# Attention's first batch sent in halves of heads, stacks gathered by term, and a new order of its first stages

## The reference, cut to what matters

```python
qkv = hidden_states @ w_attn + b_attn
q, k, v = jnp.split(qkv, 3, axis=-1)
scores = jnp.einsum('bqhd,bkhd->bhqk', q, k) * SCALE
scores = jnp.where(causal[None, None], scores + bias[None], -jnp.inf)
attn = jax.nn.softmax(scores, axis=-1)
out = jnp.einsum('bhqk,bkhd->bqhd', attn, v).reshape(B, S, HIDDEN)
return out @ w_proj + b_proj
```

## Time and profile before

| what | value |
|---|---|
| median of three runs | 691.1 us (690.16 to 693.39) |
| the profiled execution's own time | 689.53 us |
| its span, first to last instruction | 687.8 us |
| PE busy | 647.3 us, 94% of the span |
| DVE, ACT, POOL busy | 482.1, 343.7, 86.5 us |
| mean granted TensorE clock | 0.995 of full speed |
| chain that ended last | PE 77%, DVE 15%, ACT 3%, DMA 1% |

### The profile page before, as it was taken

How to read it: one execution, slowest core, us unless ns; L and a number is a source line. 1 busy time by engine, 2 the same in 40 slices (tenths; PEclk the granted TensorE clock), 3 DMA queues, 4 the chain that set the end, 5 groups by cost and what they waited for, 6 DMA issues and landing times.

```text
span 687.8 us, 10297 instructions
## 1 busy us (share of the span) xinstructions
PE 647.3 (94%) x3848; PEld 490.8 (71%) x3848; DVE 482.1 (70%) x913; ACT 343.7 (50%) x539; POOL 86.5 (13%) x185
## 2 busy tenths in 40 slices
PE   4888999999998799999998999999999899999997
PEld 4866678678676577877787675766857565788876
DVE  6755685795689789886797556465374797787565
ACT  5213554614633764423479897476384904445221
POOL 4411002102100021101042010000100310000000
PEclk9999999999999999999999999999999999999999
DMA  8395513413644130000260000000003106000000
GB/s 278 109 262 169 155 32 96 131 54 94 224 146 169 66 140 26 0 1 1 92 225 13 1 0 1 0 1 0 1 0 117 67 1 229 2 31 16 15 31 32
DMA packets 31908, 52.15 MB, mean 76 GB/s; under 512 B 3449, under 2 KB 17148, under 8 KB 30303
## 3 DMA queue, kind: packets, MB, share of 16 engines
q1 hardware_dynamic: 31282, 49.84, 22.4%
q10 hardware_dynamic: 576, 1.64, 1.0%
HBM read 42.87 MB, written 8.40 MB: 75 GB/s over the span
## 4 chain that ended last, share of the span: by engine, by line
PE 77%; DVE 15%; ACT 3%; DMA 1%; issue 1%; ACTq 1%; POOL 1%; SPq 0%; DVEq 0%; POOLq 0%
PE ps L2021 15%; PE ps L1857 13%; PE ps L1890 12%; PE ps L2089 11%; PE ps L1720 5%; DVE nmax L1100 3%; PE ps L1798 2%; PE ps L1736 2%; PE ps L1866 2%; PE ps L1700 2%; DVE nmax L1097 2%; PE ps L1788 2%; DVE prodT L1623 2%; ACTq L508 1%; PE ps L1859 1%
## 5 line engine op out<-in xcount | busy, mean ns | idle before, releaser
L2089 PE MATMUL ps<-wdT,prodT 128*128 128x512 f32 (+1 forms) x176 | 77.7, 597 | 0.4
L2089 PEld LDWEIGHTS ps<-wdT,prodT 128*128 128x128 f32 (+1 forms) x176 | 32.8, 190 | 40.7 <-issue 38.3
L817 ACT ACTIVATE probsT<-ps 128x1536 f32<-128x1536 f32 x32 | 46.2, 1450 | 28.1 <-PE ps L1788 27.9
L859 ACT ACTIVATE funs<-ps 128x512 f32<-128x512 f32 x16 | 9.5, 596 | 92.0 <-PE ps L1859 80.6
L683 POOL TENSOR_SCALAR ln_spread<-ln_moments 128x1 f32<-128x1 f32 x24 | 7.5, 310 | 283.1 <-DVE ln_moments L1171 283.0
L1177 DVE SCALAR_TENSOR_TENSOR junk<-x_sb,gate_row 128x512 f32<-128x512 f32 x48 | 41.2, 858 | 1.0
L1623 DVE COPY prodT<-ps 128x512 f32<-128x512 f32 (+1 forms) x24 | 13.7, 599 | 37.0 <-PE ps L2076 36.7
L1440 DVE SCALAR_TENSOR_TENSOR x_sb<-b_row,coef,x_sb 128x512 f32<-128x512 f32 x48 | 38.0, 792 | 1.8
L1100 DVE TENSOR_REDUCE nmax<-ps 128x4 f32<-128x1024 f32 x32 | 38.9, 1214 | 0.0
L989 ACT ACTIVATE sign_junk<-mlp_size_next,minus_guess 128x1376 bf16<-128x1376 f32 x24 | 34.6, 1443 | 0.8
L989 ACT ACTIVATE sign_junk<-mlp_size_main,minus_guess 128x1376 bf16<-128x1376 f32 x24 | 34.6, 1442 | 0.7
(11 more groups left out here) (302 smaller groups left out, 1726.9 us busy)
## 6 DMA issues: line engine op xcount, KB each, us to landing
cuts<-parts SPq DMA_DIRECT2D x16, 384.0 KB, 2.8
qst<-cuts SPq DMA_DIRECT2D x48, 128.0 KB, 2.7
w_first_raw<-in_L_ffn_w SPq DMA_DIRECT2D x6, 1024.0 KB, 7.5
w_second_raw<-in_L_ffn_w SPq DMA_DIRECT2D x6, 1024.0 KB, 8.6
kst<-cuts SPq DMA_DIRECT2D x36, 128.0 KB, 2.6
wqkv_raw<-in_L_attn_a_w_attn SPq DMA_DIRECT2D x3, 1024.0 KB, 7.9
wdT<-in_L_attn_b_w_down SPq DMA_DIRECT2D x1, 2560.0 KB, 10.0
wg_raw<-in_L_attn_b_w_gate SPq DMA_DIRECT2D x1, 2048.0 KB, 8.4
```

Of the source, the lines that this page charges most:

```text
L817: nc.scalar.activation(probsT[:, g % 2, :].rearrange("p (k n) -> p k n", k=3), slot[g % 2], ACT.Exp).then_inc(exp_ok.sem, 1)
L2089: last = nc.tensor.matmul(ps[:, Y_BANK, :], prodT[0:m, c, :], wdT[0:m, c, :], start=(c == 0), stop=(c == IC - 1))
```

## The change

The first batch's steps go in the order f = 0, 1, 2, 3, so that both sides of the first half of the heads come first. SP writes and gathers that half while the second is still being cut; ACT issues no gathers any more. The columns of q and k are ordered so that a pair of heads lies side by side, and a row in DRAM has 1024 bytes where it had 512. The writes of q are three DMAs with a broadcast source, which put part 0 three times, part 1 twice and part 2 once (768 KB for a half); k is written once (384 KB). The gather of q is then one DMA to 96 partitions (768 KB), that of k three, to 48, 32 and 16 partitions (384, 256, 128 KB). So each half has four writes and four gathers, where it had two and twelve; this holds for all batches.

The transposed rows get two sets of buffers, by odd and even batch, so `turn_rows(1)` goes ahead of the values of batch 0 (into PSUM banks 0 and 1), and `turned_part(1, 1)` goes between the groups 1 and 2 of the first batch's scores. `residue(1, 0)` and `residue(1, 1)` go behind the maxima of groups 1 and 3. `cut_biases` and its DMAs go behind the values and the gathers of batch 0. Core of the diff:

```diff
+TERM_RUNS = [(0, 3, 0), (3, 2, 1), (5, 1, 2)]
...
-    turned = np.arange(D).reshape(2, H // 2, HD).transpose(0, 2, 1).reshape(D)
+    turned = np.arange(D).reshape(2, H // 4, 2, HD).transpose(0, 2, 3, 1).reshape(D)
...
-        cuts_out = [sig(f"cuts_out{half}", 16 * 2) for half in range(2)]
-        SCATTERS = 2 * len(TERMS)
+        WRITES = 1 + len(TERM_RUNS)
+        cuts_out = [sig(f"cuts_out{half}", 16 * WRITES) for half in range(2)]
+        SCATTERS = 1 + len(TERM_RUNS)
         scat = [sig(f"scat{half}", 16 * SCATTERS) for half in range(2)]
...
-        cuts = nc.dram_tensor("cuts", (2, 2, 3, D // 2, S), BF16, kind="Internal").ap()
+        q_cuts = nc.dram_tensor("q_cuts", (2, len(TERMS), P, 2 * S), BF16, kind="Internal").ap()
+        k_cuts = nc.dram_tensor("k_cuts", (2, 3, P, 2 * S), BF16, kind="Internal").ap()
...
+        def write_side(eng, b, half, side):
+            need(eng, part3, b, 2 * half + side + 1)
+            if side == 1:
+                eng.dma_start(k_cuts[half].rearrange("m p n -> p m n"),
+                              parts[:, 1, half].rearrange("p m g t -> p m (g t)")).then_inc(cuts_out[half].sem, 16)
+            else:
+                for t, n, part in TERM_RUNS:
+                    eng.dma_start(q_cuts[half, t:t + n].rearrange("m p n -> p m n"),
+                                  parts[:, 0, half, part].rearrange("p g t -> p (g t)").unsqueeze(1)
+                                  .broadcast_to([P, n, 2 * S])
+                                  ).then_inc(cuts_out[half].sem, 16)
+
         def send_rows(eng, b, half, side):
 
-            stack = (qst, kst)[side]
             hs = slice(half * H // 2, (half + 1) * H // 2)
-            for t, term in enumerate(TERMS):
-                eng.dma_start(stack[t:TROWS:len(TERMS), hs, :],
-                              cuts[side, half, term[side]].rearrange("(d h) t -> d h t", d=HD)
+            if side == 0:
+                eng.dma_start(qst[0:TROWS, hs, :].rearrange("r h t -> r (h t)"),
+                              q_cuts[half].rearrange("m (d h) n -> (m d) (h n)", d=HD)
                               ).then_inc(scat[half].sem, 16)
+            else:
+                for t, n, _ in TERM_RUNS:
+                    eng.dma_start(kst[t * HD:(t + n) * HD, hs, :].rearrange("r h t -> r (h t)"),
+                                  k_cuts[half, 0:n].rearrange("m (d h) n -> (m d) (h n)", d=HD)
+                                  ).then_inc(scat[half].sem, 16)
...
+            write_side(sp, 0, 0, 0)
+            write_side(sp, 0, 0, 1)
+            write_side(sp, 0, 1, 0)
+            for half in range(2):
+                if half == 1:
+                    write_side(sp, 0, 1, 1)
+                need(sp, cuts_out[half], 0, 16 * WRITES)
+                for side in range(2):
+                    send_rows(sp, 0, half, side)
             sp.wait_ge(bias_cut, 4)
             sp.dma_start(bias_cuts.rearrange("i (p n) -> p i n", p=P), bias_parts[:, :, :]).then_inc(bias_out, 16)
+            sp.dma_start(x_sb[:, 2 * TB:T, :], x_v[:, 2 * TB:T, :]).then_inc(x_rest, 16)
+            sp.dma_start(gate_row[:, :], gate_w.rearrange("d e -> (d e)").partition_broadcast(P)).then_inc(gate_in, 16)
+            sp.dma_start(gate_bias[:, :], gate_b.partition_broadcast(P)).then_inc(gate_in, 16)
+            sp.dma_start(wproj_raw[:, :, :], w_proj.rearrange("(c p) n -> p c n", p=P)).then_inc(wproj_in, 16)
...
+            cut(0, (0,))
             ln(1)
-            cut(0)
+            cut(0, (1, 2, 3))
...
-            first_part(0, 0)
-            second_part(0, 0)
-            first_part(0, 2)
-            second_part(0, 2)
-            first_part(0, 1)
-            second_part(0, 1)
-            first_part(0, 3)
-            second_part(0, 3)
-            need(act, cuts_out[0], 0, 16 * 2)
-            send_rows(act, 0, 0, 1)
-            need(act, cuts_out[1], 0, 16 * 2)
-            send_rows(act, 0, 1, 1)
+            for f in range(4):
+                first_part(0, f)
+                second_part(0, f)
...
-            cut_biases()
             attention_low(1)
             dve.wait_ge(qk_bias_scaled, 1)
             residue(0, 0)
             dve.wait_ge(x_next, 16)
             ln_moments_of(1)
+            residue(0, 1)
             attention_low(2)
+            ln_rows(1)
             residue(0, 2)
-            ln_rows(1)
-            residue(0, 1)
+            for j in range(TB):
+                turned_rows_high(1, j)
             residue(0, 3)
             dve.wait_ge(bias_v_in, 16)
-            for j in range(TB):
-                value(0, j)
-            for j in range(TB):
-                turned_rows_high(1, j)
+            value(0, 0)
             for j in range(TB):
                 turned_rows_low(1, j)
-            residue(1, 0)
-            residue(1, 1)
+            value(0, 1)
+            cut_biases()
             dve.wait_ge(ranks_set, 3 * E)
...
+            def first(g):
+                if g == 1:
+                    residue(1, 0)
+                elif g == 3:
+                    residue(1, 1)
+
             for b in range(B - 1):
-                maxima(b, lambda g: steady(b, g) if b >= 1 else None)
+                maxima(b, first if b == 0 else lambda g: steady(b, g))
...
-                    if b >= 1:
+                    if b == 1:
+                        need(pe, hT_low, 0, j + 1)
+                    elif b >= 2:
                         need(pe, v_out, b - 1, j + 1)
...
-                elif b >= 1:
+                elif b == 1:
+                    need(pe, v_out, 0, f + 1)
+                elif b >= 2:
                     need(pe, hT_low, b, f + 1)
...
-            for f in turned_order(0):
+            for f in range(4):
                 turned_part(0, f)
+            turn_rows(1)
             for j in range(TB):
                 value(0, j)
-            turn_rows(1)
-            for f in range(2):
-                turned_part(1, f)
+            turned_part(1, 0)
             pe.wait_ge(alibi_in, 32)
             pe.wait_ge(consts, 11)
             for g in range(NG):
+                if g == 2:
+                    turned_part(1, 1)
                 scores(0, g)
```

More of the change, by code:

```diff
@@ L515, in row_banks @@
         def row_banks(b):
[L516 removed]
+            return first_rows if b <= 1 else work
         def row_bank(n):
@@ L553, in write_cuts, with gather @@
                 for side in range(2):
-                    need(sp, part3, b, place(b, 2 * half + side) + 1)
-                    sp.dma_start(cuts[side, half].rearrange("m (g p) t -> p (m g) t", p=P),
-                                 parts[:, side, half].rearrange("p m g t -> p (m g) t")
-                                 ).then_inc(cuts_out[half].sem, 16)
-            def gather(b, half, sides=range(2)):
+                    write_side(sp, b, half, side)
+            def gather(b, half):
                 need(sp, sT_ps, b - 1, (half + 1) * GHALF)
-                need(sp, cuts_out[half], b, 16 * 2)
-                for side in sides:
+                need(sp, cuts_out[half], b, 16 * WRITES)
+                for side in range(2):
                     send_rows(sp, b, half, side)
@@ L669, in ln, with cut @@
                 nc.gpsimd.tensor_tensor(rstd[:, :], spread[:, :], neg_half[:, :], ALU.pow).then_inc(rstd_ok.sem, 1)
-            def cut(b):
-                for k, f in enumerate(turned_order(b)):
+            def cut(b, steps=range(4)):
+                for f in steps:
                     side, pair = f % 2, f // 2
-                    need(pool, part2, b, k + 1)
-                    r = resid[:, k % 2, :].rearrange("p (h t) -> p h t", h=2)
+                    need(pool, part2, b, f + 1)
+                    r = resid[:, f % 2, :].rearrange("p (h t) -> p h t", h=2)
                     nc.gpsimd.tensor_tensor(parts[:, side, pair, 2, :, :], r,
@@ L779, in first_part @@
                 side, pair = f % 2, f // 2
-                need(act, cuts_out[pair], b - 1, 16 * 2)
-                need(act, tr_ps, b, place(b, f) + 1)
+                need(act, cuts_out[pair], b - 1, 16 * WRITES)
+                need(act, tr_ps, b, f + 1)
                 if b == 0 and f == 0:
@@ L1699, in value @@
                     for c in range(KC):
-                        last = nc.tensor.matmul(work[j], rows[:, c, at_j], weight[:, 2, c, :],
+                        last = nc.tensor.matmul(work[j], rows[b % 2][:, c, at_j], weight[:, 2, c, :],
                                                 start=(i == 0 and c == 0), stop=(i == 2 and c == KC - 1))
@@ L1720, in turned_part @@
                             last = nc.tensor.matmul(turn_bank(b, f)[:, m * S:(m + 1) * S], weight[:, side, c, columns],
-                                                    rows[:, c, :], start=(i == 0 and c == 0),
+                                                    rows[b % 2][:, c, :], start=(i == 0 and c == 0),
                                                     stop=(i == 2 and c == KC - 1))
```

57 lines of the change are left out of this document (24 added, 33 removed).

## The result

The changed kernel takes 692.34 us, the median of 22 runs (690.55 to 695.32), against 690.93 (687.73 to 693.39) for the kernel before, run on the same chip. The ratio is 1.0024, 95% interval 1.0013 to 1.0036: a loss of 0.24% or 1.7 us (the two medians differ by 1.4), inside the range and inside the 0.5% band, but a loss, where "no change" was forecast. The profiled execution took 690.55 us (span 688.8, granted clock 0.994) against 689.53 (687.8, 0.995); it is the fastest of the 22, so the trace shows the changed kernel at its best.

The account below looks back on a forecast made before the run. PE was taken to bound from the second batch on, DMA queues then DVE's maxima in the first. E moves from 57.6 to 57.5 and nothing follows: median 691.0, set at 690.8 us; range from 688.3 less half a us to 692.5 and a little.

Parts of the forecast that it names:

- S: Start of the first batch's first scores: forecast 39.1 us, bounds 38.1 and 39.7, against 41.92 before.
- E: End of the first batch's last maxima on DVE: S + 18.4 = 57.5 us, bounds 55.6 and 58.8, against 57.6 before.
- The clock: PE's 3.5 us idle ahead of S brings 3.4 us at half clock, costing 1.7 us of work, 0.9 in E.
- The second half's stacks: Half 2's gathers land at about 48.5 us; second half's first scores (group 4), wanted near 49, wait nothing or up to 1.
- Rival 2: Gathers to adjacent rows run slower: data 10.8 us, S 43.8, E 62.2, about 697 us, slower by 0.8%; chance 0.06.
- Rival 1: The merged gather runs faster, above 320 GB/s: data 4.9 us or less, S 37.6, E 55.1, time 688.3 us; chance 0.2.
- Rivals 3 and 4: 3: maxima's DMA queues behind larger writes, 1.5 us, 692.5 us, chance 0.1; 4: values stay ahead of all scores, certain.

Follow-up runs that it names:

- run 10: Run 8 with step and residues between the scores as in the changed kernel, plus 24 useless matmuls in PE's idle time ahead of them; 687.38 us, ratio 0.9965.
- run 8: Changed kernel with old stacks, half 1 gathered before half 2's writes (issued by ACT), step and residues ahead of the scores; 686.54 us, 0.9950 of the kernel before.
- Run 13: Changed kernel with 38 useless matmuls added in PE's idle time ahead of the first scores; 693.90 us, 1.0056 of the kernel before.
- run 11: Run 8 with the changed kernel's stacks (three writes of q, four gathers of adjacent rows a half); 692.79 us, 1.0032 of the kernel before.
- run 15: Run 8 with each gather of 16 rows going to adjacent partitions instead of ones six apart; 706.92 us, 1.0242 of the kernel before.
- run 12: Run 8 with half 1's k gathered from ACT's queue and half 2's k written from SP's; 690.67 us, 1.0000 of the kernel before.
- run 1: Changed kernel with the second half's write of k moved from SP's queue to ACT's; 690.98 us, a single time.
- run 3: Changed kernel with batch 1's step and residues back ahead of scores and maxima, and half 2's k written from ACT's queue; 693.13 us, 1.0044 of the kernel before.
- run 5: Changed kernel's new order alone, with the old stacks (q written once, twelve gathers a half); 690.81 us, 1.0010 of the kernel before.
- run 7: Changed kernel with SP issuing all writes, half 2's k included, ahead of the first half's gather; 695.08 us, a single time.
- run 14: Run 5 with 24 useless matmuls added in PE's idle time ahead of the first scores; 690.13 us, 0.9995 of the kernel before.
- run 2: Changed kernel with batch 1's projection step back ahead of the first scores and its residues ahead of the maxima; 693.52 us, a single time.

## Why the prediction was wrong

**Right.** The first scores, forecast for 39.1 us, came at 39.43, though two errors cancelled: the writes were through by 30.8 instead of 31.8, and the gather took 7.5 us instead of 6.1, so that it came this near is partly luck. PE was idle 5.09 us and not 3.5, its step having ended at 34.3 and not 35.6. In the front POOL's cut of f = 1 is drawn out beside DVE's `attention_low` as forecast (2.49 us from 21.54), but ends at 24.0 and not 25.0; the gathers are issued from 29.08 (29.4). The lower clock came behind the idle time and lasted the 3.4 us named, in spite of the longer idle time. The part from S to E at the full clock, 17.5 us, is 17.60 in run 10. Behind E nothing was added: the maxima go at 60.90, 1.9 us behind E (forecast 2.0). The later batches are as long as before.

**Wrong.** E was to be 57.5 and is 58.98. The 1.5 us divide so: S 0.3; the clock 0.8; the second half's landing 0.3.
- *The clock* was taken at 0.9 us, with the reason that "part lies in DVE's shadow". Without the 0.31 us of the later wait S to E is 19.24, so it cost 1.7, all of the 3.4 us at half speed and just above the bound I gave (1.6). This term is the largest miss in E. No shadow was left: scores at half speed delay DVE's first maxima (2.4 us behind S instead of 1.4 in run 10), and the step behind them delays group 2 (DVE idle 1.16 us instead of the 0.6 forecast).
- *The second half's stacks* were to land at 48.5 us, the wait ahead of group 4 "nothing or up to 1 us". They landed at 50.62, the wait was 2.27. Only 0.3 us of it shows in E, but this is the step that missed by the most, 2.1 us, and matters most, because it makes a second bound: E can't be before 50.66 + 8.3 = 58.98, however early S, even at the full clock. (8.3 is group 4 to E in run 8, 45.49 to 53.81.) Run 13 took the clock's fall out of the first half and gained nothing; run 11 took the clock's fall and the work between out of the first half and lost as much as the change. The write of k landed at 40.12 instead of 39.5, the gather moved 1.57 MB in 8.6 us (41.07 to 49.64), 184 GB/s, and not at the rate of the first, assumed 6.1.
- *Rival 2*, adjacent rows, had 0.06 and a price of 697 us. Its mechanism was at work in k's gathers alone: 703 ns a packet, where 447 and 562 were my bounds, both from rows of scattered gathers; q's 530 lie inside them. The data took 7.5 and 8.6 us, not the 9.6 from which this rival decides, so as priced it didn't come. At its full size the mechanism takes transfers of 16 rows, 943 ns (run 15). The Trainium skill's "SBUF — State Buffer", "Door 1: The DMA port swizzle", puts partitions p and p + 32 on one port; worked out by its table, 16 adjacent rows reach 4 ports of 16, 48 reach 8 and 96 all. The order of the packet times agrees: 943 ns for 16 rows a transfer, 703 for k's three, 530 for q's 96. That ports are the reason is not shown by these runs; that the place of the rows is, is.
- *Rival 1* didn't come: 768 KB and what is behind it moved at 209 GB/s (192 packets in 7.5 us) and 184, not at 320 or more. The Trainium skill's "DMA: Bandwidth & Descriptors", "Bandwidth", has 341 GB/s for 1 MB; the measurement decides, for gathers to these rows. (This rival's S of 37.6 us, and the bound of 38.1, reckon the writes through by 31.5 us, where the sum has 31.8.)
- *Rivals 3 and 4*: no delay of the maxima's DMA; and the values do stay ahead of the scores.

So the expected gain went like this: 2.5 us won at S; 1.7 given back at half clock, because PE's step had left the place where it covered the gather; 1.8 by what now stands between S and E, above all the two residues (S + 17.5 for S + 15.7, as forecast); and 0.3 by half 2's landing, a new bound so close behind the others that repairing those alone gains nothing. The sum is 3.8, of which 2.5 had been won.

## What to carry to other kernels

When work is taken from ahead of a wait, ask what else will be late at the next one: here two chains ended within 0.3 us of each other, and 0.5% was gained only by the version that shortened both (half 1 gathered before half 2's writes, step and residues back in the gather's shadow, the old stacks). Here four large gathers issued at once held up a write behind them by 6 to 7.5 us on either queue: what a later gather needs is best issued ahead of them. Before gathers are merged, look at which partitions each one reaches, and spread the rows of a small one.

## What the runs showed of the hardware

- The place of 16 rows in a stack, side by side or six apart, makes a packet of 8 KB 943 or 448 ns (the latter with engines busy 62% of the time), at full engines 147 GB/s against 231 to 239, and the kernel 2.96% slower (706.92 / 686.54, on two chips; 2.93% by the ratios).
- A write of 384 KB that lands in 2.7 us from an idle queue took 4.1 us beside gathers issued one each 0.63 us (run 8), 5.8 in run 12, 8.67 behind four large ones on its queue, and 10.2 and 9.4 behind them on the other queue (runs 1, 11).
- Idle spells of PE of 2.5 to 6.8 us were mostly followed by 3.4 to 10.2 us at the lower of the two clock levels: 2.50 by 3.4 (run 3), 5.09 by 3.4 (changed), 3.10 by 6.8 (run 5), 6.82 by 10.2 (run 7); but 3.15 us in run 14, ahead of group 4, and 2.41 in run 2, ahead of S, by none. Whether it comes and how long it lasts didn't follow the length of the idle time alone, and 2.8 us of loss for 6.8 us is near the half that the two levels give. Useless matmuls in the idle time can be worth something: 1.7 to 2.4 us in run 10, but nothing in 13, where the fall only moved.
- The mean granted clock tells runs of one kernel apart: of the changed kernel's 22, the four fastest (690.55 to 691.13 us) have 0.994, and all six with 0.989 lie between 692.80 and 694.95. One spell of 3.4 us at half speed is 0.0025 of that mean.
